# A recurrent stage with unread matmuls between its waits, one pre-activation bank, and four gates in one TanH

## What is computed

```python
x = x + _L0_xattn_ref(_layernorm(x), ctx_1024, ctx_1024, 0, mask_SxS2_ff0)
x = x + _L0_ffn_ref(_layernorm(x), ...)
x = x + _L1_xattn_ref(ctx_1024, _layernorm(x), ..., _lenS2)   # the recurrence
x = x + _L1_ffn_ref(_layernorm(x), ...)

def step(carry, tgt):                                # 256 times, one after the other
    s, c, alpha = carry
    f = conv(alpha, conv_w)
    e = einsum('a,bta->bt', va, tanh(enc_proj + (s @ Wa_s.T)[:, None, :] + einsum('bft,af->bta', f, Wa_f) + ba))
    e = where(mask, e, -1e30)
    alpha_new = softmax(e)
    g = einsum('bt,btd->bd', alpha_new, hbatch)
    rec = tgt @ L_ys.T + s @ L_ss.T + g @ L_gs_w.T + L_gs_b
    ig, fg, cg, og = split(rec, 4)
    c_next = _sig(fg) * c + _sig(ig) * tanh(cg)      # _sig(z) = tanh(z / 2) / 2 + 1/2
    s_next = _sig(og) * tanh(c_next)
```

## Time and profile before

| | |
|---|---|
| runs | 1772.58, 1774.41, 1777.65 us; median 1774.41 |
| span of the profiled execution | 1777.0 us |
| loop, from the first L1193 to the last L1243 | 445.2 to 1603.7 us |
| a step | 4.52 us |
| PE busy | 1506.0 us (85%) |
| DVE busy | 919.2 us (52%) |
| ACT busy | 528.9 us (30%) |
| POOL busy | 387.5 us (22%) |

### The profile page before, as it was taken

One profiled execution on the slowest core, in us unless ns is written; L12 is line 12 of the kernel. 1 busy time (PEld: TensorE's weight loads), 2 busy tenths in 40 slices (PEclk: granted clock), 3 DMA queues, 4 the chain that ended last, 5 costly groups with the idle time before them and its releaser, 6 DMA issues.

```text
span 1777.0 us, 43152 instructions
## 1 busy us (share of the span) xinstructions
PE 1506.0 (85%) x15683; PEld 1022.2 (58%) x15683; DVE 919.2 (52%) x4293; ACT 528.9 (30%) x2023; POOL 387.5 (22%) x1030
## 2 busy tenths in 40 slices
PE   6547999999888888888888888888888888887999
PEld 3334454544666666666666666666666666664443
DVE  4996643331555555555555555555555555553422
ACT  1342231221333333333333333333333333331211
POOL 3344321220000222222222222222222222222211
PEclk7658999999555555555555555555555555555999
DMA  8330000001200000000000000000000000000000
GB/s 326 141 115 11 1 1 0 1 1 52 77 0 0 0 0 0 0 0 0 0 0 0 0 0 0 0 0 0 0 0 0 0 0 0 0 0 1 1 24 25
DMA packets 17363, 34.51 MB, mean 19 GB/s; under 512 B 7476, under 2 KB 8675, under 8 KB 17332
## 3 DMA queue, kind: packets, MB, share of 16 engines
q1 hardware_dynamic: 17332, 34.10, 5.3%
HBM read 32.00 MB, written 2.10 MB: 19 GB/s over the span
## 4 chain that ended last, share of the span: by engine, by line
PE 62%; DVE 25%; issue 6%; ACT 5%; POOL 1%; DVEq 1%; SPq 1%; DMA 0%; POOLq 0%; ACTq 0%
PE bank L1243 18%; PE bank L1073 11%; PE bank L1193 6%; PE bank L1088 6%; PE bank L1221 5%; ACT eh L960 4%; DVE interT L746 4%; PE bank L1199 4%; DVE krep L764 3%; PE bank L1213 3%; DVE rinv L755 3%; DVE rs L743 2%; DVE g L760 2%; PE bank L1231 2%; DVE gat L771 2%
## 5 line engine op out<-in xcount | busy, mean ns | idle before, releaser
L1243 PE MATMUL bank<-krep,uh 128*128 128x128 f32 x1024 | 313.1, 461 | 23.6
L1243 PEld LDWEIGHTS bank<-krep,uh 128*128 128x128 f32 x1024 | 237.4, 320 | 92.4 <-DVE krep L764 92.4
L493 POOL TENSOR_TENSOR sscale<-ex,rinv 128x8 f32 x256 | 51.3, 200 | 667.6 <-DVE rinv L755 667.6
L1221 PE MATMUL bank<-eh,krep 128*128 128x4 f16 x2048 | 95.3, 168 | 92.5 <-ACT eh L960 92.5
L764 DVE TENSOR_TENSOR krep<-inv,ahn 128x128 f32<-128x128 f32 x512 | 162.2, 356 | 0.0
L1073 PE MATMUL bank<-xT,wbig 128*128 128x512 f16 x672 | 157.2, 386 | 3.7 <-DVE xT L591 3.7
L743 DVE TENSOR_TENSOR rs<-bank,rin 128x8 f32<-128x8 f32 x256 | 42.8, 167 | 198.1 <-PE bank L1199 198.1
L1221 PEld LDWEIGHTS bank<-eh,krep 128*128 128x128 f16 x2048 | 74.1, 105 | 114.0 <-ACT eh L960 114.0
L963 ACT ACTIVATE xs<-gat 64x8 f32<-64x8 f32 x256 | 53.4, 208 | 288.7 <-DVE gat L771 288.7
L955 ACT ACTIVATE interT<-bank 128x128 f16<-128x128 f32 x256 | 71.2, 278 | 216.9 <-PE bank L1193 216.9
L1181 PE MATMUL bank<-enc,identb 128*128 128x128 bf16 x771 | 128.4, 303 | 0.0
(11 more groups left out here) (201 smaller groups left out, 3044.5 us busy)
## 6 DMA issues: line engine op xcount, KB each, us to landing
wbig<-d_gate_qT SPq DMA_DIRECT2D x4, 896.0 KB, 10.1
wbig<-d_up_qT SPq DMA_DIRECT2D x4, 896.0 KB, 20.7
wbig<-d_down_qT SPq DMA_DIRECT2D x1, 3584.0 KB, 30.5
d_out<-x_sb SPq DMA_DIRECT2D x8, 256.0 KB, 2.0
sscale<-d_gate_sT SPq DMA_DIRECT2D x2, 896.0 KB, 8.6
interT<-d_gate_sT SPq DMA_DIRECT2D x2, 896.0 KB, 14.9
sscale<-d_up_sT SPq DMA_DIRECT2D x2, 896.0 KB, 4.2
interT<-d_up_sT SPq DMA_DIRECT2D x2, 896.0 KB, 4.3
```

The source lines that it names most:

```text
L1221: ins = mm(bank[4][:, 4 * gp:4 * gp + 4], hg2[:, j, h, gp * P:(gp + 1) * P], e[:, 4 * h:4 * h + 4], start=(first and gp == 0 and j == 0 an ...
L1243: mm(bank[1 - par][:, 0:P], uh[:, h, :], qv[:, h, :, :], start=False, stop=False, skip_group_check=True)
```

## The change

1. **One pre-activation bank.** The context part, the state part, the q part and both tanhs use bank 0 in both steps. Bank 1 is no longer read in the loop.
2. **Unread matmuls in the loop.** `keep_busy(n)` multiplies the identity with n columns of `hg2` into bank 1, which nobody reads. It stands in five places of a step, with 256, 256, 768, 768 and 768 columns (a matmul of 512 and one of 256 where it is 768), 2816 in all: ahead of the wait for the tanh, of the wait for `th_lo`, of the wait for `eh`, of the wait for q0, and after the q matmuls, ahead of the next step's wait for the state.
3. **Unread matmuls at the entry.** Sixteen of 512 columns into bank 1, between the last matmul of the second block's gates input and the loop's first masks.
4. **Gates on the same partitions.** `gat` is [64, 16]. DVE makes it with two instructions of [64, 8]. ACT takes one tanh of [64, 16] in place of two of [64, 8], into `xs`, which is 20 columns wide now. `tfi` is gone, and `ab` reads both factors from `xs`.

```diff
-        gat = sb("gat", [P, 8])
+        gat = sb("gat", [J, 16])
-        tfi = sb("tfi", [J, 8])
-        xs = sb("xs", [J, 2, 12])
+        xs = sb("xs", [J, 2, 20])
...
-                    nc.vector.tensor_tensor(gat[:], g1[:], rs[:], ALU.add).then_inc(s["g_ready"], 1)
+                    nc.vector.tensor_tensor(gat[:, 0:8], g1[J:P, :], rs[J:P, :], ALU.add)
+                    nc.vector.tensor_tensor(gat[:, 8:16], g1[0:J, :], rs[0:J, :], ALU.add).then_inc(s["g_ready"], 1)
...
-                    nc.vector.scalar_tensor_tensor(ab[:], tfi[:], 1.0, xs[:, par, 0:8], ALU.add, ALU.mult).then_inc(s["ab_ready"], 1)
+                    nc.vector.scalar_tensor_tensor(ab[:], xs[:, par, 12:20], 1.0, xs[:, par, 0:8], ALU.add, ALU.mult).then_inc(s["ab_ready"], 1)
...
-                    nc.scalar.activation(th_hi, bank[par][:, 0:P], ACT.Tanh).then_inc(s["th_s"], 1)
-                    nc.scalar.activation(th, bank[par][:, 0:P], ACT.Tanh).then_inc(s["th_full"], 1)
+                    nc.scalar.activation(th_hi, bank[0][:, 0:P], ACT.Tanh).then_inc(s["th_s"], 1)
+                    nc.scalar.activation(th, bank[0][:, 0:P], ACT.Tanh).then_inc(s["th_full"], 1)
...
-                    nc.scalar.activation(xs[:, par, 4:12], gat[J:P, :], ACT.Tanh, scale=0.5)
-                    nc.scalar.activation(tfi[:], gat[0:J, :], ACT.Tanh, scale=0.5).then_inc(s["tg_ready"], 1)
+                    nc.scalar.activation(xs[:, par, 4:20], gat[:], ACT.Tanh, scale=0.5).then_inc(s["tg_ready"], 1)
...
+            for _ in range(16):
+                mm(bank[1][:], x_part[0][:, 0, 0:P], x_part[0][:, 0, :], start=True, stop=True)
...
+            def keep_busy(n):
+                mm(bank[1][:, 0:n], identb[:], hg2[:, 0].rearrange("p h g -> p (h g)")[:, 0:n], start=True, stop=True)
...
+                    keep_busy(256)
                     pe.wait_ge(s["th_s"], l + 1)
...
+                    keep_busy(256)
                     pe.wait_ge(s["th_lo_ready"], l + 1)
...
+                    keep_busy(512)
+                    keep_busy(256)
                     pe.wait_ge(s["eh_ready"], l + 1)
...
                     masks()
-                    context_part(1 - par)
+                    context_part()
+                    keep_busy(512)
+                    keep_busy(256)
                     for h in range(2):
                         pe.wait_ge(s[f"q{h}_ready"], l + 1)
-                        mm(bank[1 - par][:, 0:P], uh[:, h, :], qv[:, h, :, :], start=False, stop=False, skip_group_check=True)
+                        mm(bank[0][:, 0:P], uh[:, h, :], qv[:, h, :, :], start=False, stop=False, skip_group_check=True)
+                    keep_busy(512)
+                    keep_busy(256)
```

More of the change, by code:

```diff
@@ L1176, in masks, with context_part @@
                 mm(bank[3][:, 0:8], etl[:], etr[:], start=True, stop=False, skip_group_check=True)
-            def context_part(par):
+            def context_part():
                 for j in range(3):
-                    mm(bank[par][:, 0:P], identb[:], enc3[:, j, :], start=(j == 0), stop=False, skip_group_check=True)
+                    mm(bank[0][:, 0:P], identb[:], enc3[:, j, :], start=(j == 0), stop=False, skip_group_check=True)
+            def keep_busy(n):
+                mm(bank[1][:, 0:n], identb[:], hg2[:, 0].rearrange("p h g -> p (h g)")[:, 0:n], start=True, stop=True)
             masks()
-            context_part(0)
+            context_part()
             with pe.Fori(0, S // 2) as i:
@@ L1192, in _ @@
                         pe.wait_ge(s["sl_ready" if st is sl else "sh_ready"], l + 1)
-                        last = mm(bank[par][:, 0:P], was2[:, j, :], st[:].unsqueeze(2).broadcast_to([J, B, TH]),
+                        last = mm(bank[0][:, 0:P], was2[:, j, :], st[:].unsqueeze(2).broadcast_to([J, B, TH]),
                                   start=False, stop=(st is sl), skip_group_check=True)
```

## The result

The changed kernel takes 1924.95 us, the median of 4 runs (1918.48 to 1929.90), against 1774.27 us for the kernel before: a ratio of 1.085, with a 95% interval of 1.082 to 1.088. It is slower by 151 us where the prediction had it 13 us faster, and the time lies outside the range.

The account below looks back on a forecast made before the run. The chain of waits from reciprocal to reciprocal, 4.53 us a step with TensorE's clock at 0.50, was taken to bound the kernel. Terms -7.0 - 6.7 + 2.4 - 1.7 = -13.0 us gave 1761.4 us, range 1717 to 1830.

Parts of the forecast that it names:

- I take it that it stays at 1.00 in the loop: TensorE's clock in the loop: assumed to hold at 1.00 (2.4 GHz), where it had been 0.50.
- rival B: Clock falls and rises inside the loop; +1.27 us per low step, 1826 us with a fifth of steps low; chance 0.27.
- there are unread matmuls in every gap: PE's work in the loop: argument that the added matmuls in all gaps speak against the clock falling.
- The rule on idle gaps: TensorE's clock: skill-page rule that it drops with idle gaps between bursts and stays up without; taken as no certainty.
- +0.09 for the added DVE instruction: Gates on DVE: the second instruction for gat moves the spreads back by 0.09 us.
- rival C: POOL goes first in all 224 later steps, ab at its late bound, +0.21 for +0.08 a step: 1790.5 us; chance 0.06.
- The clock's gain, -0.09 and -0.02 on the path: Deciding path: -0.09 us from the matmul on sl to ACT L955, -0.02 from there to the next reciprocal.
- The 0.03 that the first 32 steps were to have to spare: First 32 steps: 0.03 us the state's path had to spare against L1243, counted into a gain of 0.22 a step.
- Unread matmuls hidden at the high clock: Gaps of PE in the loop: unread matmuls fit at 1.00, 0.02 us to spare behind q1; taken as 0, up to +0.10.
- one of the signs of being wrong: Listed sign: a chain through the unread matmuls into L1193, meaning they are too long behind q1.
- Rival A: State free of POOL: all 256 steps gain 0.22 us, 1718.8 us in all; chance 0.11.
- Entry and exit, +2.4 and -1.7: Sixteen matmuls ahead of the loop cost +2.4 us; first matmuls behind it, at the high clock, give -1.7 us.

Follow-up runs that it names:

- e1: The kernel before with the change's gates alone (gat in two halves, one TanH), no unread matmuls, two banks: 1860.66 us.
- e3: The changed kernel with 3648 unread columns a step in place of 2816, the added ones ahead of the waits for th_lo, eh and el: 1797.87 us.
- e2: The changed kernel with the gates of the kernel before (gat in one instruction, two TanHs): 1795.62 us.
- e4: The changed kernel with 3648 unread columns a step in place of 2816 and the gates of the kernel before: 1753.21 us.
- e10: e9 with POOL's three pieces of a step held back by waits until the state has been written: 1745.89 us.
- e11: e10 with one TanH over 128 partitions in place of two over 64, gat still one instruction, cell state on partitions 64 to 127: 1734.31 us.
- e5: The kernel before with gat made by two instructions that stay on their partitions, 64 to 127 first, two TanHs as before: 1859.25 us (one run).
- e12: e5 with the two halves of gat in the other order, partitions 0 to 63 first: 1890.49 us.
- e8: e4 with POOL's pieces L511 and L517 made to wait for the second spread: 1791.85 us.
- e9: e4 without the sixteen unread matmuls at the entry: 1754.17 us.
- e6: The kernel before with one pre-activation bank and the sixteen unread matmuls at the entry, none in the loop, old gates: 1777.49 us.

## Why the prediction was wrong

**The step that failed: "I take it that it stays at 1.00 in the loop".** That is the larger part, 122 of the 153 us between the forecast's span (1764.0) and the measured one (1916.7). It was rival B that came true, and it had 0.27. Its price was right in kind, and near in size partly by luck: a step at the low clock took 5.63 us against the 4.50 of the forecast, +1.13, and 5.51 against 4.30, +1.21, where the prediction had +1.27. Of the +1.13 the unread matmuls are 0.76 (after less e1), where the prediction had 1.2 for them; the other 0.37 are the gates at the low clock (4.87 in e1 against 4.50), which B's price didn't hold. What was too low is how many steps pay: it reckoned with a fifth, 51, and 131 of 255 pay wholly or in part. The range ended where that fifth ended, so it left out what the trace gave no reason to exclude. I read "there are unread matmuls in every gap" as support; the gaps were filled by columns counted at the high clock, but none of the rows said how much filling is enough. The kernels after and e3 show that 832 columns more were enough, and e2 and e3 that the shown busy time doesn't tell it.

**The rule on idle gaps.** The prediction drew on the Trainium skill's page "TensorE: Matmul & The Clock Gate" (Why this matters for your kernels), by which the clock drops with idle gaps between bursts and not without, and gave it no certainty. The runs bear that doubt out: in the high step above PE waited 0.32 us ahead of L1255, its longest wait there, and the clock fell 38 times in such a loop. What the prediction didn't do is to draw the consequence, and to give B the larger chance.

**The gates, "+0.09 for the added DVE instruction".** This term was mis-sized by a mechanism it didn't have. Offsets from the reciprocal's end, medians in us:

| | before, first 32 / later | after, first 32 / later |
|---|---|---|
| `gat`, first instruction | 0.24 / 0.24 | 0.31 / 0.31 |
| `gat`, second | - | 0.48 / 0.48 |
| first spread | 0.32 / 0.33 | 0.57 / 0.69, 0.67 |
| `ab` | 0.90 / 0.90, 0.93 | 0.97 / 1.09, 1.08 |
| `sl` | 1.78 / 1.80, 1.80 | 1.84 / 2.03, 1.95 |

The first spread moved by 0.24 and 0.35 us in place of 0.09, since neither half of `gat` overlaps with what stands ahead of it. In the first 32 steps `ab` lost 0.07 where I had it gain 0.08, so that a step took 4.47 us at the high clock and not 4.30. In the others the state lost 0.19 on average where I had 0.08. That is near rival C's +0.21: POOL did go first in all 224 steps, though it held up the second `gat`, not the first spread as C had it, and in first steps the new cell too, which waited for a late `ab` that the cast had stretched. C's 1790.5 us is close to what this change gives at a held clock, 1797.9 in e3. At 0.06 its chance was too small; the argument against it, that all of L517's 0.52 us would have to be its own, looked at how long POOL takes and not at how late the spread would come.

**The clock's gain, -0.09 and -0.02 on the path.** Right. From the matmul on `sl` to the end of the next reciprocal the old gates take 2.51 us at the low clock and 2.41 at the high one (e4), and steps of 4.52 become 4.42. The 0.03 that the first 32 steps were to have to spare was 0.01 (`sl` waited 0.07 us for its matmul there, 0.06 in the others), so they become 4.40.

**Unread matmuls hidden at the high clock.** Right. In the high step above, the matmul on `sl` follows `sl` by 0.06 us, and in e4's second steps, the tightest, too. At the low clock they were the chain, one of the signs of being wrong that the prediction named.

**Rival A**, a state free of POOL, did not come by itself: the moved spreads ran free (0.48 us), but the `gat` ahead of them waited in their place. e10 reaches that state by moving POOL.

**Entry and exit, +2.4 and -1.7.** The entry was near: from the start of the last sixteen matmuls of the gates input (L1111; L1110 in after) to the loop's first mask it is 3.2 us in before and 5.4 in after, +2.2, and the same two lengths stand in every kernel without the burst and with it. The first reciprocal comes only 1.2 us later than before, since those sixteen began 1.0 us earlier in after. The exit's gain did not come: the part behind the loop was as long as before (175.0 and 175.2 us). The first matmuls there took 2.98 us against 3.64 in the earlier trace rows, and the clock had fallen again just before them, at 1743.0 us.

**Two small slips in the working.** The upper end of the forecast's range, 0.07 us in each of 256 steps above 1761.4, is 1779 and not 1778. The 1.3 us that the entry's sum takes off stand for 1.18 us of idle time in the earlier trace rows. Together they move the forecast by 0.1 us and the range's end by one.

## What to carry to other kernels

Unread work for the sake of a clock is only worth something if the clock holds in every step; a clock that comes and goes makes that work the critical path at its dearer price (a fifth of the span here), so look at the clock's slices first, add columns until the loop's are all 9 (here 832 in the stretch of few columns did it), and only then judge the rest. On VectorE, cutting an instruction into two halves of the partitions can cost far more than the added instruction (here 0.24 us on the first spread where 0.09 was reckoned), because the halves begin on different partitions (0 and 64) and don't overlap; a wider operation over all partitions (e11) gave the saving that the split one lost. And when another engine's work is moved away from one collision, list every two-input VectorE instruction between its old and its new place, the short ones too.

## What the runs showed of the hardware that I had not expected

- Two VectorE instructions in a row of which one begins on partition 0 and the other on 64 don't overlap: 0.31 in place of 0.24 us behind the reciprocal for the first half of `gat`, and 0.48 for the second; with the lower half first 0.24, 0.41, and 0.60 for what follows (e5, e12).
- A VectorE instruction of 4 or 8 columns with two inputs in SBUF waits out a GpSimd piece of the weights (it reads SBUF too) that started before it: 0.16 becomes 0.28 (`gat` in after), 0.15 becomes 0.34 (e8). A GpSimd instruction that isn't held up is shorter than the earlier trace rows show it: L517 0.39 in place of 0.52, L511 0.35 in place of 0.41.
- The granted clock fell with PE shown busy for 1075 of 1080 us (e2) and held with 1008 (e3). What in the work decides it stays open; no run here varied where the 832 columns stand or how few of them suffice.
- A loop that holds the clock also got it back by itself, and one step paid for its fall (5.3, 5.1 and 5.3 us in e9, e10 and e11, in place of 4.4).
- Sixteen dense matmuls ahead of a loop without unread work didn't keep the clock up: it fell within the loop's first step and a half and stayed at 0.50 (e6).
